# A fused conditioned residual on one Trainium2 core: the head before the quad loop laid out anew

## The chip, the cores and the metric

The kernel runs on one core of one Trainium2 chip. The metric is the device time of one execution in microseconds (us); a lower time is better. The time before is 364.88 us, the median of three runs (363.96 to 365.1).

## What is computed

`x` is 128 x 128 x 512 (batch b, position n, feature d), `cond` is 128 x 512. All numbers are float32.

```
u      = gelu(cond @ W_proj + b_proj)                 # exact gelu, 128 x 512
logits = (u @ W_u)[:, None, :] + einsum('bnd,dc->bnc', x, W_e)
out    = x + logits                                   # weight_matrix = [W_u ; W_e]
```

So each position n is one tile: the 128 x 512 slice of all batches at n, times a 512 x 512 matrix, plus a bias that depends on the batch alone (`bias` = u @ W_u). The kernel adds the identity to W_e first, so that `x @ (W_e + I)` holds the residual.

## The kernel before, in words

**Two parts.** The first eight positions are the head: four chunks of two tiles, each a plain product. The other 120 positions are 30 quads of four tiles. A quad is computed by one level of Strassen's scheme (Winograd's form): seven half-size products `m1` to `m7` in place of eight. The blocks of the left factor are a11, a12 (together `a_up`), a21 and a22, and the sums s1 to s4; the right factor's blocks are parts of W_e + I and the sums `t_sum`.

**Precision.** Every product is made in three passes from a rounded part (`hi`, `w_hi`, `t_hi`) and the rest (`lo`, `w_lo`, `t_lo`): hi x hi, hi x lo, lo x hi. ScalarE writes the rounded parts. The rests are subtractions, on VectorE (DVE) or GpSimd (POOL).

**The transposes.** TensorE needs the features of x on the partitions. A DMA brings x so that 32-row groups of partitions hold the four groups of 128 features, and VectorE's 32 x 32 transposes (line 476) do the rest. They read runs of 32 neighbouring elements and write elements four apart. Which feature stands in which block j is a free choice so long as the rows of W_e are loaded in the same order: partition (q, k) of block j holds feature 128q + 32j + k.

**The order by hand.** Each engine has one queue with its program written out, and engines wait for each other by semaphores.

- SP (lines 230 to 247) issues the loads: chunk 0, half of W_e, chunk 1, cond, W_proj, b_proj, chunk 2, W_u, chunk 3, quads 0 and 1. The other half of W_e is issued by ScalarE (line 347). Then come the stores of the head, and from line 249 the loads and stores of the quads.
- POOL makes the identity, adds it to W_e when all four parts have landed (line 293), forms `t_sum` and `t_lo` (lines 299 to 307), the rests of chunks 2 and 3 (line 312), adds the bias to the first two tiles (line 336), and then prepares quads (`prepare`, lines 314 to 331).
- ACT rounds, makes the gelu (line 368), and seeds the PSUM banks of each quad with the bias (`seed_a` line 409, `seed_c` line 417).
- DVE (lines 545 to 570) turns chunks, splits W_e (lines 548 and 552), evacuates chunks (lines 491 and 561), turns quad 0 (line 562) and combines it (line 569). Quad 1 is turned in the first `period`, behind chunk 3's evacuation.
- PE (lines 597 to 660) runs five products of zeros, chunk 0 in the order in which the parts of W_e come (line 603), the transposes of cond (line 594), chunk 1 (`plain`, lines 627 to 629), h = cond @ W_proj as 16 products that are 128 columns wide (line 642), chunk 2, the bias product (line 653) and chunk 3. Then it runs `period` after `period`, each 84 products of 256 columns (lines 666 to 670).

The first product of quad 0 (`m1`) waits for `up_lo` from POOL and `a_seeded` from ACT.

## Time and profile before

| | before |
|---|---|
| median of 3 runs | 364.88 us (363.96 to 365.1) |
| the profiled execution | 365.44 us |
| its span | 363.5 us |
| PE busy | 344.3 us (95% of the span) |
| POOL busy | 284.7 us (78%) |
| DVE busy | 250.2 us (69%) |
| ACT busy | 238.9 us (66%) |

The span runs from the first to the last instruction of the core; the execution's own time is 1.94 us longer. Times in the trace count from the span's start. In the strip of 40 slices, each 9.1 us long, PE is at nine tenths or more from the fourth slice on, but for the sixth and seventh (7 and 9) and the last; the slices before stand at 2, 6, 7.

### The profile page before, as it was taken

Reading aid. Unit: us, or ns where it says so; the run is one execution under the profiler, and the core shown is the slowest. Engines: PE = TensorE matmul, PEld = TensorE weight load, DVE = VectorE, ACT = ScalarE, POOL = GpSimd, SP = SyncE. Lnnn points to the kernel's source line nnn. Section 1 sums busy time; section 2 is a strip of 40 time slices with the busy share of each in tenths; the row PEclk is TensorE's granted clock in tenths of the full one; section 3 lists DMA queues with packets and bytes.
Section 4 is the critical chain, followed back from the end, with each engine's and each line's share of the span. In section 5 each row is a group of like instructions: output and inputs, shape, how many; then the busy total and the mean of one; then the engine's idle time right before and its main releaser. Section 6 shows DMA issues by size and latency. Waiting matters only on the chain.

```text
span 363.5 us, 7738 instructions
## 1 busy us (share of the span) xinstructions
PE 344.3 (95%) x2665; PEld 334.4 (92%) x2665; DVE 250.2 (69%) x293; ACT 238.9 (66%) x408; POOL 284.7 (78%) x201
## 2 busy tenths in 40 slices
PE   2679979999999999999999999999999999999995
PEld 0459759999999999999999999999999999999995
DVE  1884186877777777787777777778777777777811
ACT  1341426777777787777777778877777777887741
POOL 0873278998898888888888888888888898888850
PEclk9989998999999999999999999999999999999999
DMA  8996029789987787878898777888799987878214
GB/s 188 288 247 115 0 115 241 180 176 217 232 221 213 200 217 190 225 191 181 208 231 230 199 216 200 209 204 198 188 202 231 224 217 199 218 188 224 87 71 188
DMA packets 74023, 70.62 MB, mean 194 GB/s; under 512 B 2976, under 2 KB 69024, under 8 KB 69792
## 3 DMA queue, kind: packets, MB, share of 16 engines
q1 hardware_dynamic: 73728, 70.01, 77.3%
q10 hardware_dynamic: 288, 0.52, 0.5%
q8 instruction: 4, 0.07, 0.1%
q14 instruction: 3, 0.02, 0.0%
HBM read 36.96 MB, written 33.55 MB: 194 GB/s over the span
## 4 chain that ended last, share of the span: by engine, by line
PE 90%; DVE 3%; POOL 2%; DMA 2%; SPq 1%; ACT 1%; issue 0%; POOLq 0%; ACTq 0%
PE banks L666 28%; PE banks L670 28%; PE banks L668 28%; PE banks L642 2%; DMA w_e<-in_L_cond_weight_matrix 2%; DVE w_lo L552 2%; PE banks L627 1%; PE banks L629 1%; PE banks L628 1%; PE banks L653 1%; DVE lo L487 1%; SPq L222 1%; POOL y L336 1%; POOL lo L316 1%; DVE work L476 1%
## 5 line engine op out<-in xcount | busy, mean ns | idle before, releaser
L666 PE MATMUL banks<-t_hi,hi 128*128 128x256 f32 x480 | 136.0, 283 | 0.9 <-DVE y L543 0.9
L668 PE MATMUL banks<-t_lo,hi 128*128 128x256 f32 x480 | 135.8, 283 | 0.0
L670 PE MATMUL banks<-t_hi,lo 128*128 128x256 f32 x480 | 135.8, 283 | 0.0
L666 PE MATMUL banks<-w_hi,hi 128*128 128x256 f32 x360 | 102.5, 285 | 2.7 <-ACT banks L409 2.7
L476 DVE STREAM_TRANSPOSE work<-quad_raw 128x1024 f32<-128x1024 f32 (+1 forms) x60 | 95.5, 1592 | 11.2 <-POOL lo L312 9.3
L668 PE MATMUL banks<-w_lo,hi 128*128 128x256 f32 x360 | 102.4, 284 | 0.0
L670 PE MATMUL banks<-w_hi,lo 128*128 128x256 f32 x360 | 102.4, 284 | 0.0
L666 PEld LDWEIGHTS banks<-t_hi,hi 128*128 128x128 f32 x480 | 92.3, 192 | 1.1 <-issue 1.1
L668 PEld LDWEIGHTS banks<-t_lo,hi 128*128 128x128 f32 x480 | 92.3, 192 | 0.0
L670 PEld LDWEIGHTS banks<-t_hi,lo 128*128 128x128 f32 x480 | 92.1, 192 | 0.0
L316 POOL TENSOR_TENSOR lo<-work,hi 128x1024 fp32r<-128x1024 f32 x30 | 72.3, 2411 | 22.3 <-ACT hi L378 22.3
L386 ACT CAST hi<-work 128x512 fp32r<-128x512 f32 x120 | 68.7, 619 | 18.5 <-DVE work L530 8.6
L666 PEld LDWEIGHTS banks<-w_hi,hi 128*128 128x128 f32 x360 | 69.6, 193 | 3.1 <-issue 3.1
L668 PEld LDWEIGHTS banks<-w_lo,hi 128*128 128x128 f32 x360 | 69.7, 194 | 0.0
L670 PEld LDWEIGHTS banks<-w_hi,lo 128*128 128x128 f32 x360 | 69.7, 194 | 0.0
L538 DVE TENSOR_TENSOR y<-banks,snap 128x512 f32<-128x512 f32 x30 | 20.7, 692 | 45.8 <-PE banks L670 45.8
L319 POOL TENSOR_TENSOR work<-work 128x512 f32<-128x512 f32 x30 | 38.9, 1297 | 16.2 <-DVE work L530 16.2
L429 ACT COPY banks<-banks 128x512 f32<-128x512 f32 x30 | 17.1, 570 | 51.8 <-PE banks L670 51.8
L330 POOL TENSOR_TENSOR lo<-work,hi 128x512 fp32r<-128x512 f32 x30 | 39.3, 1309 | 0.0
L327 POOL TENSOR_TENSOR lo<-work,hi 128x512 fp32r<-128x512 f32 x30 | 39.2, 1307 | 0.0
L321 POOL TENSOR_TENSOR lo<-work,hi 128x512 fp32r<-128x512 f32 x30 | 39.2, 1305 | 0.0
L324 POOL TENSOR_TENSOR lo<-work,hi 128x512 fp32r<-128x512 f32 x30 | 39.0, 1302 | 0.0
(65 smaller groups left out, 425.6 us busy)
## 6 DMA issues: line engine op xcount, KB each, us to landing
out<-y SPq DMA_DIRECT2D x31, 1024.0 KB, 4.4
quad_raw<-in_x SPq DMA_DIRECT2D x120, 256.0 KB, 5.8
head_raw<-in_x SPq DMA_DIRECT2D x16, 128.0 KB, 6.6
w_proj_sb<-in_L_cond_W_proj SPq DMA_DIRECT2D x1, 1024.0 KB, 8.2
w_u<-in_L_cond_weight_matrix SPq DMA_DIRECT2D x1, 1024.0 KB, 10.2
w_e<-in_L_cond_weight_matrix ACTq DMA_DIRECT2D x2, 256.0 KB, 3.9
w_e<-in_L_cond_weight_matrix SPq DMA_DIRECT2D x2, 256.0 KB, 5.9
out<-y SPq DMA_DIRECT2D x1, 512.0 KB, 2.6
```

Of the source, the lines that this page charges most:

```text
L316: pool.tensor_tensor(slot(lo[p], UP, 2), a_up[p], slot(hi[p], UP, 2).bitcast(F32), ALU.subtract).then_inc(up_lo, 1)
L319: pool.tensor_tensor(s4[p], a12[p], s2[p], ALU.subtract).then_inc(s4_ready, 1)
L321: pool.tensor_tensor(slot(lo[p], S2), s2[p], slot(hi[p], S2).bitcast(F32), ALU.subtract).then_inc(s2_lo, 1)
L324: pool.tensor_tensor(slot(lo[p], S4), s4[p], slot(hi[p], S4).bitcast(F32), ALU.subtract).then_inc(s4_lo, 1)
L327: pool.tensor_tensor(slot(lo[p], S3), s3[p], slot(hi[p], S3).bitcast(F32), ALU.subtract).then_inc(s3_lo, 1)
L330: pool.tensor_tensor(slot(lo[p], A22), a22[p], slot(hi[p], A22).bitcast(F32), ALU.subtract).then_inc(a22_lo, 1)
L386: act.copy(slot(hi[p], at), source).then_inc(done, 1)
L476: return dve.transpose(out_.rearrange("p j (i m) -> p m j i", m=NM), in_)
L538: dve.tensor_tensor(y[p][:, upper, right], c_bank[p], snap2[p][:, :, :], ALU.add).then_inc(c12_out, 1)
L666: pe.matmul(psum[:, t, :], a_hi[:, 2 * t + j, :], b_hi[:, j, :], start=False, stop=False, skip_group_check=True)
L668: pe.matmul(psum[:, t, :], a_hi[:, 2 * t + j, :], b_lo[:, j, :], start=False, stop=False, skip_group_check=True)
L670: last = pe.matmul(psum[:, t, :], a_lo[:, 2 * t + j, :], b_hi[:, j, :], start=False, stop=(j == T - 1), skip_group_check=True)
```

## The change

The head is laid out anew, and the loop keeps its work with another order of features.

- **Feature order.** Feature 4p + j of each tile now stands on partition p of block j. W_e is loaded in rows of that kind, four DMAs, one for each j. VectorE's transposes now read elements four apart as well as write them so. a11 and a12 become blocks that lie together.
- **Chunk 0** is loaded in its natural rows (two DMAs of 256 KB) and transposed on TensorE (`flip`, 8 transposes) into PSUM; ACT rounds it from there and DVE takes the rest.
- **Products of zeros:** six ahead of the identity's wait, and eight more behind the transposes of chunk 0.
- **The identity** is added on DVE, block by block, each when its part of W_e has landed.
- **h** is one product of 128 x 512 in four steps, behind chunk 0. b_proj is loaded as a row on all partitions (256 KB) and added on DVE. The gelu is one instruction, and u is transposed on TensorE in the middle of chunk 1. The bias product stands ahead of chunk 2 (of "the third chunk").
- **ACT's first instruction** is a gelu instead of a copy.
- **All four chunks** are evacuated with the bias by DVE; POOL's addition is gone. DVE turns and combines quad 0 behind the evacuations of chunks 0 and 1, and turns quad 1 ahead of the evacuation of chunk 3.
- **SP** loads W_u ahead of chunk 2, and loads quad 2 between the two stores of the head.

```diff
-DIRECT = 2
-WARM_UP = 5
+WARM_UP = 6
+WARM_ON = 8
...
-    w_e_dram = weight_matrix[D:2 * D, :].rearrange("(q j k) c -> q k j c", q=NQ, j=NJ)
+    w_e_dram = weight_matrix[D:2 * D, :].rearrange("(p j) c -> p j c", j=NJ)
     w_proj_dram = w_proj.rearrange("(p j) c -> p j c", j=NJ)
-    b_proj_dram = b_proj.rearrange("(p j) -> p j", j=NJ)
+    b_proj_rows = b_proj.unsqueeze(0).to_broadcast([P, D])
...
+        b_proj_sb, h, u = snap_rows[0], snap_rows[2], snap_rows[3]
...
+        direct = head_raw[:, 0:T * TILE].rearrange("p (t d) -> p t d", t=T)
+        direct_psum = [banks[2][:, t, :].rearrange("p (j b) -> p j b", j=NJ) for t in range(T)]
+
+        flip_psum = banks[3][:, 1, :].rearrange("p (j b) -> p j b", j=NJ)
+        h_psum = banks[3][:, 0, :]
+        bias_psum = banks[3][:, 0, :]
...
-        a11 = [even_odd(work[s], 0) for s in range(2)]
-        a12 = [even_odd(work[s], 1) for s in range(2)]
+        a11 = [slot(work[s], 0) for s in range(2)]
+        a12 = [slot(work[s], 1) for s in range(2)]
...
-            load_head(0)
-            for q in range(2):
-                sp.dma_start(w_e[Q * q:Q * (q + 1), :, :], w_e_dram[q]).then_inc(w_e_loaded[q], 16)
-            load_head(1)
+            for t in range(T):
+                sp.dma_start(direct[:, t, :], x[:, t, :]).then_inc(direct_loaded[t], 16)
+            for j in range(NJ):
+                sp.dma_start(w_e[:, j, :], w_e_dram[:, j, :]).then_inc(w_e_loaded[j], 16)
             sp.dma_start(cond_sb[:, :], cond).then_inc(cond_loaded, 16)
             sp.dma_start(w_proj_sb[:, :, :], w_proj_dram).then_inc(w_proj_loaded, 16)
-            sp.dma_start(b_proj_sb[:, :], b_proj_dram).then_inc(b_proj_loaded, 16)
+            sp.dma_start(b_proj_sb[:, :], b_proj_rows).then_inc(b_proj_loaded, 16)
+            load_head(1)
+            sp.dma_start(w_u[:, :, :], w_u_dram).then_inc(w_u_loaded, 16)
             load_head(2)
-            sp.dma_start(w_u[:, :, :], w_u_dram).then_inc(w_u_loaded, 16)
             load_head(3)
             load_quad(0, 0)
             load_quad(1, 1)
 
-            sp.wait_ge(first_biased, 1)
             sp.wait_ge(evacuated, 2)
             sp.dma_start(out[:, 0:QUAD, :], y[0][:, :, :]).then_inc(stored[0], 16)
+            sp.wait_ge(a22_turned, 1)
+            load_quad(2, 0)
             sp.wait_ge(evacuated, HEAD_CHUNKS)
             sp.dma_start(out[:, QUAD:2 * QUAD, :], y[1][:, :, :]).then_inc(stored[1], 16)
...
-            period(0, 0, True, False)
             period(1, 1, True, True)
...
-            pool.wait_ge(ident_ready, 1)
-            for q in range(NQ):
-                pool.wait_ge(w_e_loaded[q], 16)
-            for j in range(NJ):
-                diag = w_e[:, j, :].rearrange("p (q a k) -> p q a k", q=NQ, a=NJ)[:, :, j, :]
-                pool.tensor_tensor(diag, diag, ident[:, :].rearrange("p (q k) -> p q k", q=NQ),
-                                   ALU.add).then_inc(w_diag_ready, 1)
-
-            b_of = w_e[:, :, :].rearrange("p (j e) (h c) -> p e h j c", e=2, h=2)
+            b_of = w_e[:, :, :].rearrange("p (e j) (h c) -> p e h j c", e=2, h=2)
...
-            for c in range(DIRECT, HEAD_CHUNKS):
-                pool.wait_ge(head_hi_ready, c + 1)
+            for c in range(2, HEAD_CHUNKS):
+                pool.wait_ge(head_hi_ready, c)
                 pool.tensor_tensor(x_lo[c], x_t[c], x_hi[c].bitcast(F32), ALU.subtract).then_inc(head_lo_ready, 1)
...
-
-            pool.wait_ge(evacuated, 1)
-            pool.wait_ge(bias_copied, 1)
-            pool.tensor_tensor(y[0][:, upper, :], y[0][:, upper, :],
-                               bias[:, :].unsqueeze(1).to_broadcast([P, T, C]), ALU.add).then_inc(first_biased, 1)
             prepare(0, 0)
...
-            for q in range(2, NQ):
-                act.dma_start(w_e[Q * q:Q * (q + 1), :, :], w_e_dram[q]).then_inc(w_e_loaded[q], 16)
             act.wait_ge(zeros_ready, 1)
-            act.copy(scratch[:, :], zeros[:, 0:1]).then_inc(scratch_written, 1)
+            act.activation(scratch[:, :], zeros[:, 0:1], ACT.Gelu).then_inc(scratch_written, 1)
 
             def head_hi(c):
-                act.wait_ge(turned, c + 1)
+                act.wait_ge(turned, c)
                 act.copy(x_hi[c], x_t[c]).then_inc(head_hi_ready, 1)
 
-            head_hi(0)
+            for t in range(T):
+                act.wait_ge(direct_flipped, t + 1)
+                act.copy(x_hi[0][:, t, :, :], direct_psum[t]).then_inc(direct_hi_ready, 1)
             for j in range(1, NJ):
                 act.wait_ge(w_diag_ready, j + 1)
                 act.copy(w_hi[:, j, :], w_e[:, j, :]).then_inc(w_hi_ready[j], 1)
@@ -360,13 +357,11 @@
             for n in range(4):
                 act.wait_ge(t_summed, 4)
                 act.copy(t_hi[:, n, :, :], t_sum[n]).then_inc(t_hi_ready, 1)
+            act.wait_ge(h_ready, 1)
+            act.activation(u[:, :], h[:, :], ACT.Gelu).then_inc(u_ready, 1)
+            act.wait_ge(u_flipped, 1)
+            act.copy(u_t[:, :, :], flip_psum).then_inc(u_t_ready, 1)
             head_hi(2)
-
-            act.wait_ge(h_ready, 1)
-            act.wait_ge(b_proj_loaded, 16)
-            for e in range(NJ):
-                last = act.activation(u_t[:, e, :], h_psum[:, e, :], ACT.Gelu, bias=b_proj_sb[:, e:e + 1])
-            last.then_inc(u_ready, 1)
             head_hi(3)
 
...
-                    last = transpose(x_t[c][:, t, :, :],
-                                     head_chunk(c)[:, :, t, :].rearrange("p m (j k) -> p m j k", k=Q))
+                    last = transpose(x_t[c][:, t, :, :].rearrange("p j (i m) -> p m j i", m=NM),
+                                     head_chunk(c)[:, :, t, :].rearrange("p m (k j) -> p m j k", k=Q))
...
+                high = rows[:, :, upper, :].rearrange("p m n (k j) -> p m j (n k)", k=Q)
+                low = rows[:, :, lower, :].rearrange("p m n (k j) -> p m j (n k)", k=Q)
+                by_block = "p (j r) (i m) -> p m j (r i)"
+                if not first:
+                    dve.wait_ge(s4_ready, k - 1)
+                elif p == 1:
                     dve.wait_ge(head_lo_ready, 1)
-                else:
-                    dve.wait_ge(s4_ready, k - 1)
-                transpose(a_up[p], rows[:, :, upper, :].rearrange("p m n (j k) -> p m (n j) k", k=Q)).then_inc(
-                    up_turned, 1)
+                transpose(a_up[p].rearrange(by_block, r=T, m=NM), high).then_inc(up_turned, 1)
                 if first and p == 0:
...
                 else:
                     dve.wait_ge(s3_ready, k)
-                transpose(a21, low[:, 0]).then_inc(a21_turned, 1)
-                if first:
+                transpose(a21.rearrange(by_block, r=T, m=NM), low[:, :, 0:2, :]).then_inc(a21_turned, 1)
+                if not first:
+                    dve.wait_ge(a22_lo, k - 1)
+                elif p == 1:
...
+                transpose(a22[p].rearrange(by_block, r=T, m=NM), low[:, :, 2:4, :]).then_inc(a22_turned, 1)
...
                 if first:
-                    dve.wait_ge(t_lo_ready, 4)
+                    dve.wait_ge(t_lo_ready, 2 * p + 2)
...
-            turn_chunk(0)
-            dve.wait_ge(w_diag_ready, 1)
-            dve.tensor_copy(w_hi[:, 0, :], w_e[:, 0, :]).then_inc(w_hi_ready[0], 1)
-            direct_lo(0)
-            for j in range(NJ):
+            def add_identity(j):
+                dve.wait_ge(w_e_loaded[j], 16)
+                diag = w_e[:, j, :].rearrange("p (a r) -> p a r", r=NJ)[:, :, j]
+                dve.tensor_tensor(diag, diag, ident[:, :], ALU.add).then_inc(w_diag_ready, 1)
+
+            def split_direct(t):
+                dve.wait_ge(direct_hi_ready, t + 1)
+                dve.tensor_tensor(x_lo[0][:, t, :, :], direct_psum[t], x_hi[0][:, t, :, :].bitcast(F32),
+                                  ALU.subtract).then_inc(direct_lo_ready, 1)
+
...
+            dve.wait_ge(ident_ready, 1)
+            add_identity(0)
+            dve.wait_ge(w_diag_ready, 1)
+            dve.tensor_copy(w_hi[:, 0, :], w_e[:, 0, :]).then_inc(w_hi_ready[0], 1)
+            split_direct(0)
+            add_identity(1)
+            split_direct(1)
+            add_identity(2)
+            add_identity(3)
+            for j in range(NJ):
+                split_w(j)
+            dve.wait_ge(cond_flipped, 1)
+            dve.tensor_copy(cond_t[:, :, :], flip_psum).then_inc(cond_ready, 1)
             turn_chunk(1)
-            direct_lo(1)
-            dve.wait_ge(cond_flipped, 1)
-            dve.tensor_copy(cond_t[:, :, :], cond_psum).then_inc(cond_ready, 1)
+            dve.wait_ge(head_hi_ready, 1)
+            dve.tensor_tensor(x_lo[1], x_t[1], x_hi[1].bitcast(F32), ALU.subtract).then_inc(direct_lo_ready, 1)
+            dve.wait_ge(h_summed, 1)
+            dve.wait_ge(b_proj_loaded, 16)
+            dve.tensor_tensor(h[:, :], h_psum, b_proj_sb[:, :], ALU.add).then_inc(h_ready, 1)
             turn_chunk(2)
             turn_chunk(3)
-            dve.wait_ge(multiplied, 1)
-            dve.tensor_copy(y[0][:, upper, :], banks[0][:, :, :]).then_inc(evacuated, 1)
-            turn_quad(0, 0, True)
             dve.wait_ge(bias_summed, 1)
             dve.tensor_copy(bias[:, :], bias_psum).then_inc(bias_copied, 1)
             dve.wait_ge(bias_copied, 1)
             dve.tensor_tensor(bias_step[:, :], bias_psum[:, right], bias[:, left], ALU.subtract).then_inc(bias_ready, 1)
+            evacuate(0)
             evacuate(1)
+            turn_quad(0, 0, True)
+            combine_quad(0, 0, True)
             evacuate(2)
-            combine_quad(0, 0, True)
+            turn_quad(1, 1, True)
             evacuate(3)
...
-                    turn_quad(k + 1, 1 - p, early)
+                    if not early:
+                        turn_quad(k + 1, 1 - p, early)
                     combine_quad(k + 1, 1 - p, early)
...
+            def warm(count):
+                for _ in range(count):
+                    pe.matmul(banks[3][:, 0, :], zeros[:, 0:P], zeros[:, :], start=True, stop=True)
+
+            def flip(psum, cols, done):
                 for j in range(NJ):
-                    last = pe.transpose(psum[:, j, :], rows.rearrange("b (p j) -> b j p", j=NJ)[:, j, :], ident[:, :])
+                    last = pe.transpose(psum[:, j, :], cols[:, j, :], ident[:, :])
                 last.then_inc(done, 1)
...
+                return rows.rearrange("b (p j) -> b j p", j=NJ)
+
             pe.wait_ge(zeros_ready, 1)
+            warm(WARM_UP)
             pe.wait_ge(ident_ready, 1)
-            for _ in range(WARM_UP):
-                pe.matmul(banks[3][:, 0, :], zeros[:, 0:P], zeros[:, :], start=True, stop=True)
-
-            def product(psum, a, b, j, first=False, last=False):
-                return pe.matmul(psum, a[:, j, :], b[:, j, :], start=first, stop=last)
+            for t in range(T):
+                pe.wait_ge(direct_loaded[t], 16)
+                flip(direct_psum[t], by_j(direct[:, t, :]), direct_flipped)
+            warm(WARM_ON)
+
+            def product(t, a, b, j, first=False, last=False):
+                return pe.matmul(banks[0][:, t, :], a[:, t, j, :], b[:, j, :], start=first, stop=last)
 
             for j in range(NJ + 1):
                 if j < NJ:
                     pe.wait_ge(w_hi_ready[j], 1)
-                    if j == 0:
-                        pe.wait_ge(head_hi_ready, 1)
                     for t in range(T):
-                        product(banks[0][:, t, :], x_hi[0][:, t], w_hi, j, first=(j == 0))
-                    if j == 0:
-                        pe.wait_ge(direct_lo_ready, 1)
+                        if j == 0:
+                            pe.wait_ge(direct_hi_ready, t + 1)
+                        product(t, x_hi[0], w_hi, j, first=(j == 0))
                     for t in range(T):
-                        product(banks[0][:, t, :], x_lo[0][:, t], w_hi, j)
+                        if j == 0:
+                            pe.wait_ge(direct_lo_ready, t + 1)
+                        product(t, x_lo[0], w_hi, j)
+                if j == NJ - 1:
+                    pe.wait_ge(cond_loaded, 16)
+                    flip(flip_psum, by_j(cond_sb[:, :]), cond_flipped)
                 if j > 0:
                     pe.wait_ge(w_lo_ready[j - 1], 1)
                     for t in range(T):
-                        last = product(banks[0][:, t, :], x_hi[0][:, t], w_lo, j - 1, last=(j == NJ))
+                        last = product(t, x_hi[0], w_lo, j - 1, last=(j == NJ))
             last.then_inc(multiplied, 1)
-            pe.wait_ge(cond_loaded, 16)
-            flip(cond_psum, cond_sb[:, :], cond_flipped)
+
+            pe.wait_ge(cond_ready, 1)
+            pe.wait_ge(w_proj_loaded, 16)
+            for j in range(NJ):
+                last = pe.matmul(h_psum, cond_t[:, j, :], w_proj_sb[:, j, :], start=(j == 0), stop=(j == NJ - 1))
...
-            pe.wait_ge(direct_lo_ready, DIRECT)
-            *_, last = plain(1)
+            pe.wait_ge(direct_lo_ready, T + 1)
+            for t, last in enumerate(plain(1)):
+                if t == 0:
+                    pe.wait_ge(u_ready, 1)
+                    flip(flip_psum, by_j(u[:, :]), u_flipped)
             last.then_inc(multiplied, 1)
 
-            pe.wait_ge(cond_ready, 1)
-            pe.wait_ge(w_proj_loaded, 16)
-            w_proj_cols = w_proj_sb[:, :, :].rearrange("p j (d e) -> p j e d", e=NJ)
-            for e in range(NJ):
-                for j in range(NJ):
-                    last = pe.matmul(h_psum[:, e, :], w_proj_cols[:, j, e, :], cond_t[:, j, :],
-                                     start=(j == 0), stop=(j == NJ - 1))
-            last.then_inc(h_ready, 1)
+            pe.wait_ge(w_u_loaded, 16)
+            pe.wait_ge(u_t_ready, 1)
+            pe.wait_ge(h_ready, 1)
+            for j in range(NJ):
+                last = pe.matmul(bias_psum, u_t[:, j, :], w_u[:, j, :], start=(j == 0), stop=(j == NJ - 1))
+            last.then_inc(bias_summed, 1)
 
             pe.wait_ge(head_lo_ready, 1)
             *_, last = plain(2)
             last.then_inc(multiplied, 1)
 
-            pe.wait_ge(w_u_loaded, 16)
-            pe.wait_ge(u_ready, 1)
-            for j in range(NJ):
-                last = pe.matmul(bias_psum, u_t[:, j, :], w_u[:, j, :], start=(j == 0), stop=(j == NJ - 1))
-            last.then_inc(bias_summed, 1)
-
             pe.wait_ge(head_lo_ready, 2)
-            for t, last in enumerate(plain(3)):
-                if t == 0:
-                    pe.wait_ge(bias_ready, 1)
+            pe.wait_ge(bias_ready, 1)
+            *_, last = plain(3)
             last.then_inc(multiplied, 1)
...
@@ -712,16 +737,22 @@
 
             def period(k, p, first):
                 m1(k, p)
+                if first:
+                    pe.wait_ge(t_lo_ready, 1)
                 m5(k, p)
                 if not first:
                     m4(k - 1, 1 - p)
+                if first:
+                    pe.wait_ge(t_lo_ready, 2)
                 m6(k, p)
                 m2(k, p)
                 m3(k, p)
+                if first:
+                    pe.wait_ge(t_lo_ready, 3)
                 m7(k, p)
 
+            period(0, 0, True)
             pe.wait_ge(t_lo_ready, 4)
-            period(0, 0, True)
```

## Rows read from the trace of the kernel before

**Rows 1.** Busy time: loop, one period; columns length, engines, clock, DMA, GB/s.

```profile
58.00:357.00 299.00, 299.00 (x2493) 299.00 (x2493) 216.09 (x259) 221.48 (x381) 254.21 (x175) 1.00 0.80 200
...
200.00:210.08 10.08, 10.08 (x87) 10.08 (x86) 7.56 (x10) 7.56 (x14) 8.74 (x6) 1.00 0.83 201
```

**Rows 2.** PE alone by head stage: length, PE, clock, DMA share, GB/s.

```profile
13.20:20.85 7.65, 7.60 (x26) 1.00 1.09 302
20.85:23.46 2.61, 0.00 (x0) 1.00 1.21 218
23.46:30.80 7.34, 7.33 (x26) 0.77 1.22 213
30.80:38.20 7.40, 7.40 (x34) 1.00 0.22 39
...
43.60:47.10 3.50, 3.50 (x10) 1.00 0.00 0
47.10:52.50 5.40, 5.40 (x24) 1.00 0.23 99
52.50:55.24 2.74, 0.04 (x2) 0.91 0.58 236
55.24:58.00 2.76, 2.76 (x13) 0.50 1.02 306
```

**Rows 3.** The chain that ended last, 3 to 31 us: start, length, what.

```profile
4.15 6.28 DMA w_e<-in_L_cond_weight_matrix
...
13.19 5.93 DVE w_lo L552 x4
19.12 1.97 DVE work L476 x2
21.11 1.05 ACT hi L353
22.19 1.24 DVE lo L487
```

**Rows 4.** The same chain, 46 to 58 us.

```profile
47.12 0.70 DVE bias L564
...
47.96 2.41 POOL y L336
50.37 2.36 POOL lo L316
52.72 1.24 POOL work L319
...
54.51 0.59 ACT banks L409
...
55.24 0.55 PE banks L666
```

**Rows 5.** DMA issues of the first 1.2 us: size, median us to landing.

```profile
w_e<-in_L_cond_weight_matrix ACTq DMA_DIRECT2D x2, 256.0 KB, 3.9
```

**Rows 6.** Groups by line and shape: busy us, mean ns of one, idle before.

```profile
L476 DVE STREAM_TRANSPOSE work<-quad_raw 128x1024 f32<-128x1024 f32 x30 | 62.7, 2089 | 1.9 <-PE banks L629 1.9
...
L386 ACT CAST hi<-work 128x512 fp32r<-128x512 f32 x120 | 68.7, 619 | 18.5 <-DVE work L530 8.6 <-POOL work L319 7.3 <-DVE work L476 2.7
...
L476 DVE STREAM_TRANSPOSE work<-quad_raw 128x512 f32<-128x512 f32 x30 | 32.8, 1094 | 9.3 <-POOL lo L312 9.3
L476 DVE STREAM_TRANSPOSE banks<-quad_raw 128x512 f32<-128x512 f32 x30 | 22.9, 762 | 0.0
...
L530 DVE TENSOR_TENSOR work<-banks,work 128x512 f32<-128x512 f32 x30 | 20.7, 692 | 14.2 <-ACT hi L386 14.1
...
L491 DVE TENSOR_TENSOR y<-banks,bias 128x1024 f32<-128x1024 f32 x3 | 3.6, 1216 | 0.0
...
L594 PE MATMUL banks<-ident,cond_sb 128*128 128x128 f32 x4 | 0.6, 281 | 0.0
```

More of the change, by code:

```diff
@@ L69, in build_cond_residual @@
         y = [sb(f"y{s}", [P, QUAD, C]) for s in range(2)]
-        snap2 = [sb(f"snap2_{s}", [P, T, H]) for s in range(2)]
-        snap5 = [sb(f"snap5_{s}", [P, T, H]) for s in range(2)]
+        snap_rows = [sb(f"snap_rows{s}", [P, T * H]) for s in range(4)]
+        snap2 = [rows[:, :].rearrange("p (t c) -> p t c", t=T) for rows in snap_rows[0:2]]
+        snap5 = [rows[:, :].rearrange("p (t c) -> p t c", t=T) for rows in snap_rows[2:4]]
         w_e = sb("w_e", [P, NJ, C])
@@ L136, in build_cond_residual @@
         b_proj_loaded = sem("b_proj_loaded")
-        w_e_loaded = [sem(f"w_e_loaded{q}") for q in range(NQ)]
+        w_e_loaded = [sem(f"w_e_loaded{j}") for j in range(NJ)]
+        direct_loaded = [sem(f"direct_loaded{t}") for t in range(T)]
+        direct_flipped = sem("direct_flipped")
+        direct_hi_ready = sem("direct_hi_ready")
         w_u_loaded = sem("w_u_loaded")
@@ L146, in build_cond_residual @@
         cond_ready = sem("cond_ready")
+        h_summed = sem("h_summed")
         h_ready = sem("h_ready")
         u_ready = sem("u_ready")
+        u_flipped = sem("u_flipped")
+        u_t_ready = sem("u_t_ready")
         bias_summed = sem("bias_summed")
@@ L674, in b_of @@
             def b_of(w, e, cols):
[L675 removed]
+                return w[:, 2 * e:2 * e + 2, cols]
             def m1(k, p):
```

33 lines of the change are left out of this document (9 added, 24 removed).

## The prediction

> **What bounds the kernel now.** I read the busy times by window first. In the loop TensorE (PE) is busy 299.00 of 299.00 us; a period of one quad is 10.08 us, and in it DVE works 7.56, ACT 7.56 and POOL 8.74 us [rows 1]. So the loop is PE's, at the full clock, and no edit to other engines shortens it. Next I read PE alone in the head [rows 2]. From 13.2 us on it is busy but for two gaps: 20.85 to 23.46 and 52.50 to 55.24, where the quads begin. Behind both gaps the granted clock is the lower level, 1.2 GHz: the stage from 23.46 shows a mean of 0.77 and takes 7.34 us for the 24 products that take 5.40 at 2.4 GHz (47.10 to 52.50), and 55.24 to 58.00 shows 0.50. Last I read the chain of waits. In the first gap it runs through DVE and ACT [rows 3]; in the second through POOL and ACT [rows 4].
>
> Everything after the first product of quad 0 is a fixed tail: 363.5 - 55.24 = 308.26 us, of which 55.24 to 58.00 ran at half clock and so holds 2.76 / 2 = 1.38 us that go if the clock stays up. The question is when quad 0 begins; I call that S. It is 55.24 now.
>
> **Up to chunk 1.** Chunk 0's transposes leave DVE. PE needs 8 transposes, 0.6 us per four at full clock [rows 6]; they wait for loads of 256 KB that land about 3.9 us after issue [rows 5], the second near 5.3 us, and their cover is W_e, which comes later. In SP's queue the last part of W_e is the sixth issue, as before, where it landed at 10.43 [rows 3]; ahead of it lie the same 1.5 MB, now without short packets. Landing 3.9 us after issue it would be there at 8. DVE's own work from the first part on is: four identity additions (128 elements each; bounds 0.2 and 0.5 us, I take 0.4 since they are short but strided), one rounding (0.66 before, taken as the 0.69 of a 512-wide operation) and two splits from PSUM (0.69 each, [rows 6]), 3.6 us from 5.9, so 9.5 us. The bounds are 8.5 and 10.9. Then come the four splits of W_e, 5.93 us [rows 3]. I don't make them cheaper: POOL forms `t_sum` beside them as before. That gives 15.4; PE's chunk 0 is behind the last split by two products and costs nothing. The eight extra products of zeros end at about 9 us; chunk 0 can't start much before that anyway, and its 5.4 us fit ahead of 15.4.
>
> Now DVE copies cond's transposes (0.7), turns chunk 1 (1.97), ACT rounds it (1.05), DVE takes the rest (1.24) [rows 3]; with 0.1 of hand-overs chunk 1 starts at 20.5 against 23.46. Four SP issues now lie ahead of chunk 1's loads that were behind (cond, W_proj, b_proj, the fourth part of W_e came from ACT). 3.5 MB must land by 16.1: 1.5 MB by at most 10.43 and 2.1 million bytes at 302 GB/s [rows 2] give 17.4 as the late bound; I take 15 to 16, no wait, since the first 1.5 MB come sooner. h runs on PE inside these 4.4 us: a product of 512 columns in four steps, 3.5 us like the bias product in [rows 2], in place of 7.40. It is thus off the path; it covers none of DVE's work, so nothing is late if it takes a us more.
>
> **From chunk 1 to the quads, PE.** Chunk 1 takes 5.4 us, u's transposes 0.6, the bias 3.5: it is summed at 30.0 (47.10 before). The gelu is ready less than one us ahead of u's transposes, which stand at 23.2 in the middle of chunk 1: DVE adds b_proj (0.7) behind the rest of chunk 1, ACT does `t_hi` behind its rounding of chunk 1 (from 19.2, four of 0.62 [rows 6]) and then the gelu (0.6), 22.3. SP's load of b_proj grows from 2 to 256 KB, 1.2 us at 218 GB/s for all later loads; quad 0's data, by that count at about 33, are wanted at 33.7. That cover is thin. Chunks 2 and 3 follow at 10.8 us, to 40.8. POOL has their rests ready: `t_lo`, four of about 1.3, ends near 26, then come two of 2.41 [rows 4], 28.4 and 30.8, for chunks that begin at 30.0 and 35.4.
>
> **From the bias to the quads, DVE.** The order by hand is the new bound. From 30.0: the bias and its step (0.70 + 0.5), two evacuations (2 x 1.2), turning quad 0 (2.09 + 0.76 + 1.09 = 3.9), three combining operations (2.05) [rows 4, 6]: 39.6. Then POOL forms s4 (1.24), ACT rounds it (0.62) and seeds (0.59), and 0.2 to start [rows 4]: S = 42.2. PE, done at 40.8, waits 1.4 us. What goes for good: POOL's addition of 2.41 us and the 2.36 behind it [rows 4], which now have DVE's combining beside them. For a wait that is added: DVE stands at the evacuation of chunk 3 only after turning quad 1, and `seed_a` of quad 1 on ACT waits for that, until 39.6 + 1.2 + 3.9 + 1.2 = 45.9. Behind it on ACT stand quad 1's rounding of s1 and the copy `snap2` that m7 of quad 0 waits for; PE comes to m7 at 42.2 + 5 x 1.44 = 49.4. I cost it at nothing, with two us of cover. SP's load of quad 2 stands ahead of the second store and goes out at 37.9 when the raw buffer is free; it is wanted behind quad 1's combining, near 50.
>
> Does the clock fall in a gap of 1.4 us? The gaps of 2.61 and 2.74 us were followed by the lower level; none as short as 1.4 is in the trace. Bounds 0 and 1.4 us; I take 0, for the gap is half as long.
>
> **The transposes in the loop.** They now read four elements apart. No row shows such a read on DVE. The write side does: 512 elements into SBUF take 1094 ns and into PSUM 762, and the step from 512 to 1024 elements costs 995 ns, against 524 for an evenly laid operation (1216 - 692) [rows 6]. So a strided side can cost 0.47 us per 512. If the read overlaps the write, only the transposition into PSUM grows, by at most 0.33 to 0.47 us; a period then has 8.0 us of DVE, and nothing is lost. If it adds up, a quad costs 4 x 0.47 = 1.9 us more. Below nothing there is no gain. I take the overlap: two streams, each at two steps per element.
>
> The Trainium skill (SBUF — State Buffer, Door 1: The DMA port swizzle) says that SBUF is read in lines of 16 bytes and that each access on a new line pays a penalty. The write side agrees here, 1094 against 762 ns; for reads no row shows it. By that rule with penalties in sequence the time would be the third case below.
>
> **The sum.** S = 42.2; 42.2 + 308.26 - 1.38 = 349.1 us of span; 1.94 outside it give 351.0 for an execution like the profiled one. The median of the runs shown is 0.56 below that execution, which gives 350.5. I forecast 350.8. A measurement of this kernel can tell about 0.3%, 1.1 us.
>
> **The rivals.**
>
> 1. *The clock falls or loads come late in the head.* For: both gaps before led to it, chunk 1's and quad 0's loads have covers near nothing, and chunk 0 is fed by splits with pauses of over an us. One fall costs 1.4 (quad start) to 1.9 us (7.34 - 5.40), a late chunk 1 up to 1.3. Time 352 to 354. Against: PE's gaps add up to less than before. Chance 0.25.
> 2. *The strided read adds to the strided write, at the write's price.* Chunk 1's turning adds 0.9 and quad 0's 1.9: S = 45.0. A period has 7.56 + 1.9 on DVE and its wait for ACT of 14.1 / 29 = 0.5 [rows 6]: 9.95 of 10.08, no slack. Time 353.6, up to 357 if some periods slip. For: the same memory serves both. Chance 0.12.
> 3. *DVE becomes the bound of the loop: slower.* The point is 10.08 - 7.56 - 0.5 = 2.0 us more per quad. From there each us costs 30; above 2.4 the gain of 14 us is gone. If each transposition doubled (+3.9 us), the loop would add 30 x 1.9 = 57 and S 4.9: about 413 us. For: the write stride alone costs about two steps per element. Against: that needs twice the write's price. Chance 0.07.
> 4. *The change doesn't do what it says:* quad 0 waits as long as before, 2.7 us behind chunk 3, and nothing of the DVE order helps. PE is still there earlier: S = 43.5, with the clock down 353.7. Chance 0.04, within the first case's range.
>
> My forecast, 349 to 352, has 0.5. What is left, 0.02, is no difference for a cause I don't see. Faster by over 0.3%: 0.5 + 0.25 + 0.12 + 0.04 = 0.91, less what may be hidden, 0.90; within 0.3%: 0.02; slower: 0.08. The range goes from 348.8 (S = 40.8, PE never waits, less the median's difference) to 356, which takes in the first, fourth and most of the second case.
>
> **What would show it.** The first loop product near 42 us; DVE's `w_lo` ending at 15.4; the bias product ending at 30; a gap of 1.4 us ahead of the first loop product that ends with ACT's seed; a full clock from chunk 1 on; transpositions at 2.09, 1.09 and 0.8 to 1.2 us; PE without idle time in the loop. The prediction fails if transpositions exceed 3 us for 1024 elements, or if PE stands for loads between 15 and 35 us.

## The result: 352.25 us, and the profile after

The changed kernel takes 352.25 us, the median of four runs (352.14 to 352.34). The kernel before took 364.42 us beside it (362.22 to 365.1). The ratio is 0.9666, with a 95% interval from 0.9628 to 0.9703. I had forecast 350.8 and a range of 348.8 to 356. The profiled execution took 352.34 us and its span is 350.4, so 1.94 us lie outside it as before.

PE alone, by stages that answer to [rows 2]; length, busy time, granted clock, DMA share, GB/s:

```profile
15.05:18.75 3.70, 3.70 (x9) 1.00 1.02 278
18.75:21.61 2.86, 0.01 (x1) 1.00 1.18 201
21.61:27.85 6.24, 6.24 (x29) 1.00 1.22 213
27.85:31.30 3.45, 3.45 (x9) 1.00 1.23 219
31.30:42.17 10.87, 10.87 (x48) 1.00 0.62 175
42.17:43.47 1.30, 0.00 (x2) 1.00 1.02 189
43.47:46.20 2.73, 2.73 (x23) 1.00 0.73 133
```

The stages are h, a wait, chunk 1 with u's transposes, the bias, chunks 2 and 3, a wait, and the first loop products. The 13.1 us of span (363.5 - 350.4) come from four places. Chunk 1 starts 1.85 us sooner (23.46 to 21.61). From there to the end of chunk 3 PE takes 20.6 us where it took 29.0: h's 7.40 us are gone from this stretch, 1.94 us of lower clock as well, and chunk 1's stage is 0.84 us longer than 5.40 (6.24): u's transposes take 0.47 of that, and the first product behind the wait takes 0.50 where the others take 0.23. The gap ahead of the quads is 1.30 us, not 2.74. The 1.38 us of lower clock behind that gap are gone: the first 2.73 us of the loop hold 23 products, where 2.76 us held 13.

The chain of waits that ended last, in the head; it answers to [rows 3, 4]; start, length, what:

```profile
7.79 9.31 DMA head_raw<-in_x
...
17.12 2.11 DVE work L471 x2
...
19.26 1.05 ACT hi L348
...
20.33 1.24 DVE lo L567
...
31.32 0.70 DVE bias L574
...
32.47 2.26 DVE y L482 x2
34.73 1.95 DVE work L471
36.68 0.98 DVE banks L471
37.66 1.01 DVE work L471
...
41.40 1.14 DVE y L482
...
42.74 0.59 ACT banks L404
```

Two things hold the head now: the landing of chunk 1's load, 17.1 us, and, from the bias on, DVE's program. The DMA row stands where [rows 3] had W_e. The chain puts the last step down to DVE's evacuation of chunk 2 (`y`, 41.40), but the seed at L404 needs only the first two evacuations. The rows of the engines show what it stood behind; start, length, and in brackets the idle time before and what ended it:

```profile
40.11 0.69 DVE L521 TENSOR_TENSOR work<-banks,work 128x512 f32<-128x512 f32 x1
...
40.88 1.30 POOL L321 TENSOR_TENSOR work<-work 128x512 f32<-128x512 f32 x1 [0.64 <-DVE work L521]
...
42.22 0.62 ACT L381 CAST hi<-work 128x512 fp32r<-128x512 f32 x1 [0.23 <-POOL work L321]
42.74 0.58 ACT L404 COPY banks<-bias 128x512 f32<-128x512 f32 x1
```

That is the path of the forecast: DVE's third combining operation, POOL's s4, ACT's rounding of it, the seed.

Ahead of this path DVE stood idle for 4.0 us, from 27.4 to 31.3, until the bias was summed. The kernel before had turned quad 0 by then, and its time from the bias to the first loop product was 8.1 us (47.10 to 55.24), against 12.2 here. The last of quad 0's loads was issued at 22.6 and took some 7 us to land, so by my estimate one to two us of the idle time could have gone to turning quad 0. No run tried that.

DVE's transposes of the quads, and one period of the loop; they answer to [rows 6] and [rows 1]:

```profile
L471 DVE STREAM_TRANSPOSE work<-quad_raw 128x1024 f32<-128x1024 f32 x30 | 63.4, 2115 | 0.0
L471 DVE STREAM_TRANSPOSE work<-quad_raw 128x512 f32<-128x512 f32 x30 | 33.7, 1124 | 0.0
L471 DVE STREAM_TRANSPOSE banks<-quad_raw 128x512 f32<-128x512 f32 x30 | 33.3, 1110 | 0.0
...
200.00:210.08 10.08, 10.08 (x86) 10.08 (x85) 8.03 (x10) 7.63 (x14) 8.76 (x6) 1.00 0.84 213
```

The two forms that write SBUF kept their length (2089 and 1094 ns before); the one that writes PSUM went from 762 to 1110 ns. DVE works 8.03 us of a period, and PE is still busy throughout.

### The profile page after: what moved, and what is told of

Its sections match the earlier page's. It is cut to its first block, busy times and chain, and to the rows that moved or that the text cites. A ratio compares the mean times of both kernels' runs of the same rounds, so it can differ in the third digit from the quotient of the medians.

```text
span 350.4 us, 7724 instructions
## 1 busy us (share of the span) xinstructions
PE 340.2 (97%) x2662; PEld 327.4 (93%) x2662; DVE 260.8 (74%) x297; ACT 239.9 (68%) x406; POOL 280.7 (80%) x196
## 4 chain that ended last, share of the span: by engine, by line
PE 89%; DVE 4%; DMA 3%; SPq 2%; ACT 1%; issue 1%; DVEq 0%; ACTq 0%
PE banks L691 29%; PE banks L695 29%; PE banks L693 29%; DMA head_raw<-in_x 3%; DVE work L471 1%; PE banks L675 1%; DVE y L482 1%; SPq L231 1%; PE banks L658 1%; PE banks L660 1%; PE banks L659 1%; SPq L242 0%; DVE lo L567 0%; ACT hi L348 0%; DVE banks L471 0%
## 5 line engine op out<-in xcount | busy, mean ns | idle before, releaser
L471 DVE STREAM_TRANSPOSE work<-quad_raw 128x1024 f32<-128x1024 f32 (+1 forms) x60 | 97.2, 1620 | 0.0
L529 DVE TENSOR_TENSOR y<-banks,snap_rows 128x512 f32<-128x512 f32 x30 | 20.8, 692 | 41.9 <-PE banks L695 41.9
L424 ACT COPY banks<-banks 128x512 f32<-128x512 f32 x30 | 17.1, 570 | 46.9 <-PE banks L695 46.9
L373 ACT CAST hi<-work 128x1024 fp32r<-128x1024 f32 x30 | 31.6, 1055 | 15.1 <-DVE work L471 15.1
L329 POOL TENSOR_TENSOR lo<-work,hi 128x512 fp32r<-128x512 f32 x30 | 39.2, 1308 | 0.0
L332 POOL TENSOR_TENSOR lo<-work,hi 128x512 fp32r<-128x512 f32 x30 | 39.2, 1306 | 0.0
L323 POOL TENSOR_TENSOR lo<-work,hi 128x512 fp32r<-128x512 f32 x30 | 39.0, 1299 | 0.0
## 6 DMA issues: line engine op xcount, KB each, us to landing
w_u<-in_L_cond_weight_matrix SPq DMA_DIRECT2D x1, 1024.0 KB, 12.2
```

The source lines that it names most:

```text
L323: pool.tensor_tensor(slot(lo[p], S2), s2[p], slot(hi[p], S2).bitcast(F32), ALU.subtract).then_inc(s2_lo, 1)
L329: pool.tensor_tensor(slot(lo[p], S3), s3[p], slot(hi[p], S3).bitcast(F32), ALU.subtract).then_inc(s3_lo, 1)
L332: pool.tensor_tensor(slot(lo[p], A22), a22[p], slot(hi[p], A22).bitcast(F32), ALU.subtract).then_inc(a22_lo, 1)
L373: act.copy(slot(hi[p], UP, 2), a_up[p]).then_inc(up_hi, 1)
L471: return dve.transpose(out_, in_)
L529: dve.tensor_tensor(y[p][:, upper, right], c_bank[p], snap2[p][:, :, :], ALU.add).then_inc(c12_out, 1)
```

## The experiments

The runs below were made on three other occasions, beside the kernel before each time; its medians there were 365.56, 364.08 and 365.05 us, against 364.42 beside the change. The change itself was measured only once. So where an edited kernel is set beside the change's 352.25 us, a difference of a us or less is not told apart, and the profiles say more than the medians.

**Where the gain comes from.** Two parts of the change were tried alone; the order on DVE, the identity on DVE and chunk 0's transposes on TensorE were not. The first puts the bias back behind chunk 2:

```diff
+            pe.wait_ge(head_lo_ready, 1)
+            *_, last = plain(2)
+            last.then_inc(multiplied, 1)
             pe.wait_ge(w_u_loaded, 16)
...
             last.then_inc(bias_summed, 1)
-            pe.wait_ge(head_lo_ready, 1)
-            *_, last = plain(2)
-            last.then_inc(multiplied, 1)
```

> The changed kernel with one part undone: the bias product stands behind chunk 2 again, as before the change. Theory (the time from the bias to the first loop product is a chain of 12.2 us on DVE, POOL and ACT that the change laid beside chunks 2 and 3): the bias is summed at 36.8 in place of 31.3, the first loop product starts at 49.0, PE stands still for 6.7 us ahead of it and its clock falls to the lower level for a stretch that costs 1.4 us more; span 357.3. Rival (PE's own work bounds the head): the span stays at 350.4 to 351, since PE's work is the same.

It took 361.39 us (median of 8, 360.3 to 362.19), 9.1 more than the change. PE alone in this kernel:

```profile
44.10:50.78 6.68, 1.58 (x8) 0.85 0.68 183
50.78:55.60 4.82, 4.82 (x22) 0.50 0.42 72
```

The bias was summed at 38.67, 1.9 us later than I gave, since chunk 2 now waited for POOL's rest. The first loop product came at 50.78, 12.1 us behind the bias. The lower clock lasted 4.8 us and more: from the first loop product to the span's end it took 309.1 us, 2.2 more than the change's 306.9, where I gave it 1.4. The later start (7.3 us) and the clock make up the 9.5 us by which this span (359.9) is longer. So with the DVE order of the change, the bias's place is worth most of the whole gain.

The second takes the kernel before and makes h's loaded weights lie together:

```diff
-            w_proj_cols = w_proj_sb[:, :, :].rearrange("p j (d e) -> p j e d", e=NJ)
+            w_proj_cols = w_proj_sb[:, :, :].rearrange("p j (e d) -> p j e d", e=NJ)
```

> The kernel before with one edit: h's 16 narrow products load their weights from 128 neighbouring columns of W_proj, not from columns four apart; so u holds permuted features and the bias is not the reference's. Theory (the strided load of weights was what made h slow): h takes 3.8 us in place of 7.4, chunk 2 and the bias come 3.5 us sooner, and since POOL's and DVE's chain behind the bias goes with them, the span falls by about 3.5 us, to 360. Rival (the narrow shape costs it): 7.4 us again, no change.

It took 360.87 us (358.6 to 362.58) against 365.05: ratio 0.9887, interval 0.9811 to 0.9963. The other side is the changed kernel with h cut into 16 narrow products again:

```diff
-            for j in range(NJ):
-                last = pe.matmul(h_psum, cond_t[:, j, :], w_proj_sb[:, j, :], start=(j == 0), stop=(j == NJ - 1))
+            for e in range(NJ):
+                for j in range(NJ):
+                    last = pe.matmul(h_psum[:, e * P:(e + 1) * P], cond_t[:, j, :],
+                                     w_proj_sb[:, j, e * P:(e + 1) * P], start=(j == 0), stop=(j == NJ - 1))
```

> The changed kernel, but h is again 16 products of 128 columns; unlike before the change the loaded weights (cond) lie together. Theory (short products in float32 cost by their count): 7.4 us as before the change, against 3.7, so h ends at 22.5 and chunk 1 starts 0.9 us later. Rival (before, the strided reading of W_proj as weights made them slow): under 4.5 us, and no change of the span.

Its one run took 351.83 us. The loads of weights for h, in the kernel before, then in the kernel before with weights that lie together, and in the changed kernel with narrow products; nanoseconds, least, median, most:

```profile
L642 PEld LDWEIGHTS banks<-cond_t,w_proj_sb x32: 308/329/332, 30.4 to 37.6; 128*128 128x128 f32 x32
```

```profile
L642 PEld LDWEIGHTS banks<-cond_t,w_proj_sb x32: 188/192/192, 31.2 to 34.7; 128*128 128x128 f32 x32
```

```profile
L653 PEld LDWEIGHTS banks<-w_proj_sb,cond_t x32: 186/192/192, 16.7 to 20.2; 128*128 128x128 f32 x32
```

Sixteen narrow products take 3.6 us wherever the weights lie together. The width of h's products bought nothing; that they no longer load W_proj four elements apart did, 3.7 us of h's time. My theory for the second of these runs falls: I expected 7.4 us.

**The gap ahead of the quads.** The change, with ACT's two seeds moved up:

```diff
+            seed_a(0, 0, True)
+            seed_c(0, 0, True)
             hi_s1(0, 0, True)
             hi_s2(0, 0, True)
             hi_s3(0, 0, True)
             hi_s4(0, 0, True)
-            seed_a(0, 0, True)
-            seed_c(0, 0, True)
```

> The changed kernel with one edit: ACT seeds quad 0's two banks ahead of its rounding of s1 to s4, not behind it. Theory (the order on ACT is what PE waits for after chunk 3): the seed's inputs are there at 34.7 us, so the first loop product starts when chunk 3 ends, at 42.3 in place of 43.5; the gap of 1.3 us goes, s2's rest comes one us later but is still early. Span 349.2, 1.2 us less than the changed kernel's 350.4. Rival (DVE's chain behind the bias bounds it anyway): the wait moves to m6, which then waits for the rest of s2, and the span stays within 0.3 us of 350.4.

It took 352.72 us (351.68 to 355.5, 5 runs): no gain that can be told. The profiled run is the slowest of the five, 355.5 us, for a reason that lies ahead of the edit: chunk 1's load landed at 19.0 us, PE waited 2.6 us for chunk 1, and the clock fell behind that wait. DVE's row, PE's wait (us in total, times, longest) and PE's stage behind it:

```profile
19.00 2.12 DVE L471 STREAM_TRANSPOSE work<-head_raw 128x512 f32<-128x512 f32 x2 [1.85 <-DMA head_raw<-in_x]
...
PE banks L658 <- DVE lo L567: 2.6, 1, 2.6
...
23.40:28.50 5.10, 4.99 (x17) 0.67 1.01 207
```

Behind that, this run has no wait ahead of the first loop product, and a new one at `m7` of quad 0, the sixth of its products to run:

```profile
53.81 0.36 PE L691 MATMUL banks<-t_hi,hi 128*128 128x256 f32 x1 [0.93 <-ACT snap_rows L441]
```

This is the wait that the prediction costed at nothing with two us of cover: ACT stands at quad 1's seed until chunk 3 is evacuated, behind quad 1's turning. When quad 0 starts sooner the cover is gone. The seed ended at 52.57 us and DVE's s1 of quad 1, which ACT rounds next, at 52.55, so two causes ended together there. Neither theory had the wait there. The same edit on the kernel before:

> The kernel before with one edit: ACT seeds quad 0's two banks ahead of its rounding of s1 to s4. Theory (in the kernel before the seed waited on ACT behind s4, which waited for POOL): the seeds are written at 50.5 us, the rest of a_up is ready at 52.7, the first loop product starts at 52.9 in place of 55.2 with no gap, and the clock stays up: span 359.7, or 361.1 if the clock falls all the same. Rival (POOL is the bound): the first product starts sooner but m6 waits for POOL's rest of s2 until 55.2, and the span is above 361.5.

It took 360.91 us (359.73 to 361.49) against 365.56; ratio 0.9897, interval 0.9819 to 0.9975. The first loop product came at 51.24. By the medians that is 4.7 us, over a third of the change's gain; between the fastest runs of either (359.73 and 361.87) it is 2.1. The profiled span is 5.0 us shorter, but 1.6 of these lie in chunk 1, which the swap doesn't touch: it ran at the full clock here, 5.70 us for 7.34. The other 3.4 us are the swap's, for the gap and the lower clock behind it went together. PE there, first the wait ahead of chunk 1 (2.15 us are idle), then chunk 1 at the full clock, then the start of the loop:

```profile
20.90:23.50 2.60, 0.45 (x5) 1.00 1.22 220
23.50:29.20 5.70, 5.70 (x26) 1.00 1.23 214
...
51.24:54.00 2.76, 2.76 (x23) 1.00 0.56 232
```

**What holds chunk 1.** The change, with the issues of chunk 1's load moved ahead of those of W_proj and b_proj:

```diff
+            load_head(1)
             sp.dma_start(w_proj_sb[:, :, :], w_proj_dram).then_inc(w_proj_loaded, 16)
...
-            load_head(1)
```

> The changed kernel with one edit: chunk 1 is loaded ahead of W_proj and b_proj. Theory (chunk 1's late landing, 17.1 us, set its start): it lands near 13, DVE turns it at 15.0, chunk 1 starts at 19.5 in place of 21.6, h still fits in front of it since W_proj lands near 15; all later steps come 2.1 us sooner and the span is 348.3. Rival (W_proj, now 1.6 us later, holds h and so the gelu): the gain is under 1 us, with PE waiting for h or for u in the middle of chunk 1.

352.1 us (352.02 to 353.07): no change; chunk 1 started at 21.28 us, 0.3 sooner. The load came in time, but W_e's splits were slow. DVE and POOL in this run:

```profile
10.49 5.76 DVE L549 TENSOR_TENSOR w_lo<-w_e,w_hi 128x512 fp32r<-128x512 f32 x4
...
10.67 1.65 POOL L301 TENSOR_TENSOR work<-w_e 128x512 f32<-128x512 f32 x1 [9.19 <-DVE w_e L540]
```

The same two in the changed kernel's profile:

```profile
10.02 2.51 DVE L549 TENSOR_TENSOR w_lo<-w_e,w_hi 128x512 fp32r<-128x512 f32 x4
...
10.22 3.46 POOL L301 TENSOR_TENSOR work<-w_e 128x512 f32<-128x512 f32 x1 [8.74 <-DVE w_e L540]
```

So two causes of nearly the same length stand side by side: with slow splits DVE is free for chunk 1 near 16.7, and its load lands at 17.1. Then the two engines were set in either order. First, DVE's splits of W_e stand behind POOL's first sum:

```diff
+            dve.wait_ge(t_summed, 1)
```

> The changed kernel, but DVE's four splits of W_e wait until POOL has written its first t_sum, so that POOL is at work when they begin. Theory (two engines take turns, and it depends on which came first): the four splits take about 6 us as in the kernel before, not 2.5, end near 17.5, and chunk 1 is turned 1.2 us later. Rival (DVE gets its way whenever it has work ready): 2.5 us again, end near 14, no change of the span.

The splits took 5.72 us, chunk 1 started at 22.45, the one run took 353.17. But slow splits were also seen in the run above, where DVE began first, so this doesn't show that the order of the start decides. Second, POOL's sums stand behind the last split, together with the earlier load of the run above:

```diff
+            load_head(1)
...
-            load_head(1)
...
+            pool.wait_ge(w_lo_ready[NJ - 1], 1)
```

> The changed kernel with two edits: chunk 1 is loaded ahead of W_proj and b_proj, and POOL begins t_sum only when DVE has split W_e. In the run with the load alone the splits took 5.7 us, in the changed kernel's 2.5. Theory (two causes of nearly the same length hold chunk 1: the landing of its load and the splits that share time with POOL): with both gone the splits end at 13, cond is copied at 14.5 to 15.2, chunk 1 starts at 19.6 and the span is 348.4. Rival (PE is next: h, 3.5 us, or the late W_proj holds the gelu): PE waits in the middle of chunk 1 for u, and the span is above 349.5.

350.73 us (350.38 to 351.46), 1.5 under the change, and the span is 1.5 us shorter too (348.9). The ratio to the kernel before is 0.9632, with an interval from 0.9561 to 0.9702 that overlaps the change's, so the gain rests on the profile and on four runs that are all under the change's four. The splits took 2.49 us and chunk 1 started at 20.0, not 19.6: PE waited 0.9 us for W_proj, now the later load. Both theory and rival had a part.

**All four edits together:** the load, POOL's wait, ACT's seeds, and on DVE the evacuation of chunk 3 ahead of quad 1's turning:

```diff
-            turn_quad(1, 1, True)
             evacuate(3)
+            turn_quad(1, 1, True)
```

> The changed kernel with four edits: chunk 1's load first, POOL behind the splits, quad 0's seeds ahead of s1 to s4 on ACT, and chunk 3 evacuated ahead of turning quad 1 on DVE. Theory: chunk 1 starts at 19.6, the bias is summed at 29.3, the first loop product starts at 40.3 when chunk 3 ends, and m7 of quad 0 finds its copy (in the run with the seeds alone it waited 0.9 us, since ACT stood at a seed that waited for chunk 3's evacuation behind quad 1's turning); span 347.2, 3.2 us under the changed kernel's. Rival (the wait only moves on to m1 of quad 1, whose rest POOL gets later): 348 to 349.

350.66 us (349.67 to 351.13, 6 runs); ratio to the kernel before 0.9627, interval 0.9574 to 0.9681. All six are under the four of the change, by 1.6 us in the median. PE's waits from 15 to 60 us, with the us in total, the times and the longest:

```profile
PE banks L692 <- ACT snap_rows L442: 0.7, 1, 0.7
PE banks L653 <- DMA w_proj_sb<-in_L_cond_W_proj: 0.7, 1, 0.7
PE banks L692 <- ACT snap_rows L433: 0.2, 1, 0.2
```

The loop starts at 39.53, when chunk 3 ends. The wait at `m7` is still there, 0.7 us: ACT's copy stands behind the rounding of quad 1's s1, and DVE makes s1 only behind both the turning of quad 1 and the evacuation of chunk 3, in whichever order they stand. The two further edits gained nothing over the pair before, 350.73.

**The transposes and DVE's slack in the loop.** The change, with `turn_quad` reading neighbouring elements:

```diff
-                high = rows[:, :, upper, :].rearrange("p m n (k j) -> p m j (n k)", k=Q)
+                high = rows[:, :, upper, :].rearrange("p m n (j k) -> p m (n j) k", k=Q)
...
-                by_block = "p (j r) (i m) -> p m j (r i)"
+                by_block = "p j (i m) -> p m j i"
...
```

> The changed kernel, but the quads' transposes read runs of 32 neighbours as before the change; the writes stay four apart. The order of the features then doesn't match W_e's, so the quads' results are those of permuted features. Theory (read and write overlap, each strided side has the same rate): the transposition into PSUM falls from 1.11 to 0.76 us, the two into SBUF stay at 2.1 and 1.1, and the span stays within 0.3 us of 350.4. Rival (the strided read costs on top): those into SBUF get shorter too.

```profile
L471 DVE STREAM_TRANSPOSE work<-quad_raw 128x1024 f32<-128x1024 f32 x30 | 62.6, 2086 | 0.0
L471 DVE STREAM_TRANSPOSE work<-quad_raw 128x512 f32<-128x512 f32 x30 | 32.9, 1095 | 0.0
L471 DVE STREAM_TRANSPOSE banks<-quad_raw 128x512 f32<-128x512 f32 x30 | 23.0, 767 | 0.0
```

Only the one into PSUM falls; the time stays, 351.83 us (351.7 and 351.96). Then two transposes that nobody reads were added for each quad from the third on:

```diff
+                if not first:
+                    dve.wait_ge(spare_done, k - 1)
+                    transpose(slot(head_raw, 0).rearrange(by_block, r=T, m=NM), low[:, :, 2:4, :])
+                    transpose(slot(head_raw, 1, 2).rearrange(by_block, r=T, m=NM), high).then_inc(spare_done, 1)
...
```

> The changed kernel with two more transposes for each quad from the third on, on DVE, 1.0 and 2.0 us, whose output nobody reads. Theory (DVE has 10.08 - 8.03 = 2.05 us left in a period): DVE becomes the bound of the loop, a period takes 11.0 to 11.5 us, and the span grows by 27 to 40 us. Rival (waits inside DVE's program make it the bound much sooner): more than 45 us.

The one run took 391.65 us. The span grew by 39.5 us to 389.9, which is 1.41 for each of the 28 quads. Of the 3.0 us added, 1.6 were free.

**The second group of zero products** left out:

```diff
-WARM_ON = 8
+WARM_ON = 0
```

> The changed kernel without the eight products of zeros behind the transposes of chunk 0. Theory (they keep the clock up for chunk 0): PE stands idle from 5.5 to 8.1 us, the clock is at the lower level for part of chunk 0, cond's transposes come later than 14.3 and push chunk 1 by 0 to 1.5 us. Rival (chunk 0 is hidden behind the splits and the load anyway): the span stays at 350.4.

356.01 us (355.71 and 356.32), 3.8 more than the change. PE in the profiled run: chunk 0, the wait, and chunk 1.

```profile
7.90:13.90 6.00, 6.00 (x14) 0.50 1.08 327
...
20.75:23.00 2.25, 0.05 (x2) 1.00 1.18 218
...
24.00:27.90 3.90, 3.90 (x14) 0.56 1.09 219
```

It lost more than I gave either theory, though only 2.1 and 3.0 us of it lie in the span (352.5 and 353.4; the rest lies outside). Chunk 0 ran at 1.2 GHz, and that alone held nothing: DVE waited 0.3 us for cond's transposes and then 1.4 us more for chunk 1's load. The 3.0 us of the profiled span are this load, which landed 1.3 us later, at 18.4, and chunk 1, which met the lower clock as well, at a cost of about 1.7 us. The edit doesn't explain the load, and the profile with ACT's seeds moved shows both things with all the products of zeros in place. Both runs of this kernel were slower than any of the change, so the second group may be worth something, but it isn't shown.

## Why the prediction was right, point by point

| step of the sum | forecast | measured |
|---|---|---|
| the last identity addition ends | 9.5 | 10.1 |
| the four splits of W_e | 5.93 | 2.51 |
| chunk 1's load lands | 15 to 16, at most 17.4 | 17.1 |
| chunk 1 starts | 20.5 | 21.61 |
| the bias is summed | 30.0 | 31.3 |
| from there to the first loop product | 12.2 | 12.2 |
| S | 42.2 | 43.47 |
| from S to the span's end | 306.9 | 306.9 |

The mechanism held: the quads wait for the hand-written order behind the bias, the clock stays up there, the loop is PE's and unchanged. Of the 1.3 us that S came late, 1.1 are one mis-sized term, chunk 1's landing; the other 0.2 lie in chunk 1's stage, 6.24 us for 6.0. I had the late bound of the landing from the rows (17.4) and took an earlier value because the first 1.5 MB would come sooner, 3.9 us after issue. The parts of W_e landed 5.4 to 6.3 us after issue. The measured wait of DVE for chunk 1 was 2.1 us. The landing also varies: in the other profiles of the changed head in which DVE waited for it, it came between 16.45 us and 19.0.

The measured 352.25 us is just above the 349 to 352 to which I gave 0.5. It lies in the 352 to 354 of the first rival, and the half of that rival that says "loads come late", with a late chunk 1 at up to 1.3 us, is what happened.

The splits were mis-sized the other way. That changed nothing in this run, since the load was later anyway. In seven other profiles of the changed head in which neither of these two engines was made to wait for the other, the four splits took 5.76 to 5.79 us, so the 5.93 was a fair value for most executions and this profile is the odd one; what that leaves open stands in the last section.

The time from the bias on was right to 0.1 us with two errors inside. I had given the transposition into PSUM 0.76 us; it took 1.07, since I had named its growth (by at most 0.33 to 0.47 us) for the loop and not for quad 0. The two evacuations came out at 2.26 us against 2.4. So DVE reached the combining 7.4 us behind the bias instead of 7.5, and from there to the first product it took 4.8 instead of 4.7.

*Clock.* I argued that a gap of 1.4 us is half as long as those that were followed by a fall. None followed it. But the longest gap of the changed head is one I had put at under a us, 18.75 to 21.61. At 2.86 us it is longer than both gaps of [rows 2], and the clock stayed up, while gaps of 2.6 us (the kernel before, and the changed kernel with the seeds moved) and 2.2 us (without the second group of zeros) were followed by a fall, and one of 2.15 us (2.60 - 0.45) in the kernel before with the seeds moved was not. What decides it was not settled, so that the clock stayed up in the result's profile is partly luck. The first rival was thus nearer than its 0.25 reads.

*The loop.* The growth of the one transposition is 0.35 us by its mean and 0.47 by DVE's busy time in a period (8.03 - 7.56), inside the bound of 0.33 to 0.47. The point at which DVE becomes the loop's bound was put at 2.0 us a quad. Beyond the 0.35 to 0.47 that the change took, 1.6 us more were free, which makes about 2.0. The slower rival's mechanism is real, and its price, double transposes, didn't come. The price of a strided side did: 343 ns for the read into PSUM (767 to 1110). Where SBUF is written four apart it hardly adds: 2086 against 2115 ns, and 1095 against 1124, without and with the strided read. The Trainium skill (SBUF — State Buffer, Door 1: The DMA port swizzle) has each access on a new line pay; for the read side the runs agree. For the write side no run shows it: the 1094 against 762 ns of the prediction set SBUF beside PSUM, both written four apart, and no transposition writes SBUF evenly. The prediction also tied penalties in sequence to its third case; by its own numbers they are the second, and the third needs twice the price.

*What I took for h* was right in the sum and wrong in the cause: I let a product of 512 columns stand for the gain, and the strided weights had been the cost.

## What to carry to other kernels

A serial chain across three engines should be priced from the event that starts it: here 12.2 us behind the bias, to be laid beside 10.9 us of products, and its place was worth 9 us with the clock that fell. Where two causes end within half a us of each other, removing one shows next to nothing; take both away together. And a wait costed at nothing should be named with its cover, because the next edit takes the cover away, as the seeds showed.

## What the runs showed of the hardware that I had not expected

- Loading float32 weights from elements four apart takes 329 ns against 192, and a narrow float32 product 0.46 us against 0.23.
- DVE's subtractions with both inputs in SBUF, beside POOL's: in one profile DVE went through all four in 2.5 us and POOL's first took 3.46; in seven others they took turns, 5.8 us and 1.65. In all eight DVE had begun about 0.2 us before POOL. The Trainium skill (SBUF — State Buffer, Who interferes with whom) says that such a pair contends, and that the order of issue decides who waits. The taking turns agrees; why POOL lost four turns in a row in the other case stays open.
- The kernel before spread over 361.87 to 366.42 us in 13 runs, with mean granted clocks from 0.999 down to 0.985. The change's four runs lie within 0.2 us at 0.999 to 1.000. Against the run of 361.87 us the change gains 9.6 us. The rest of its gain, about 2.6 us, goes with the lower mean clock, but no trace of the run of 361.87 us shows where.
